# Second layer of a four-layer mixture-of-experts network: in every other slot VectorE casts the f32 gelu to fp16 in place of a second gelu on ScalarE

## The chip, the cores and the metric

The kernel runs on one core of one Trainium2 chip. The metric is the device time of one execution in microseconds (us). The engines are TensorE (PE in the profile; PEld is its weight load), VectorE (DVE), ScalarE (ACT), GpSimd (POOL) and SyncE (SP, here only the issuer of loads).

## The reference

Sixteen images of 64 channels and 24 x 24 pixels pass four layers. Each layer is `x = x + conv(layernorm(x))`, then `t = t + ffn(layernorm(t))` on the 9216 tokens of 64 channels. Each ffn routes a token to 2 of 8 experts. The second layer's ffn, which the change touches, is

```python
weights = top_p / top_p.sum(axis=-1, keepdims=True)
xe = xn[None, :, :] * ln_g[:, None, :] + ln_b[:, None, :]
h = jax.nn.gelu(jnp.einsum('end,edh->enh', xe, W1) + b1[:, None, :], approximate=False)
y = jnp.einsum('enh,ehd->end', h, W2) + b2[:, None, :]
out = (weights[:, :, None] * sel).sum(axis=1)
```

with 256 hidden units for each of 8 experts; `sel` is the rows of `y` of the two chosen experts. The first layer's ffn has the same form with 128 hidden units. Layers three and four have experts of 682 hidden units with a silu gate.

## The kernel before

The tokens are held in two halves of 4608 (36 tiles of 128). Layers one and two are computed densely: every expert for every token, and the routing weight (zero for six experts) multiplies the result. Layers three and four gather only the chosen rows, through tables in HBM that GpSimd's indirect DMAs fill. Precision is kept by splitting: a value goes into a matmul as an fp16 part and an fp16 remainder.

The dense part (`dense(l, h)`, one function for each engine) walks over *slots*. A slot is a span of 4 tiles (512 tokens), one expert, and one chunk `c` of 128 hidden units. Layer one has one chunk, layer two has two, `c = 0` and `c = 1`, and the two slots of an expert are a *unit* (called a pair below). A half of layer two has 72 units, 144 slots. In a slot `w`:

- PE (`up`, L1732 and L1733) makes 128 x 512 hidden values in one of three PSUM banks, two slots ahead of their use.
- ACT (L848) reads the bank twice: a gelu in f32 into `hid` (the two tiles `hb0`, `hb1` in turn), and the same gelu in fp16 into `hid_hl` (four tiles in turn, `hl0`, `hl1`, `act0`, `act1`). It must first see that VectorE is done with slot `w - 2` (semaphore `lo_ready`) since `hid` has two buffers, and that PE is done with slot `w - 4` (`down_ps`).
- DVE (`low`, L1435) writes the remainder, f32 minus fp16 part, into the second half of the fp16 tile.
- PE (`down`, L1748, 12 matmuls) multiplies both parts by the second weight; with `c = 0` it adds the bias first (L1742) and starts a new sum, with `c = 1` the sum is whole.
- DVE (`gated`) multiplies the unit's sum by the routing weights (L1452, into one of two buffers), and POOL (L688) adds this to `x`. In the second half from unit 32 on (`direct`), DVE itself multiplies and adds (L1446, four instructions), since POOL then scatters rows for layer three (L635).

The order on each engine is written out. DVE does `low(k)`, and after the `low` of the next unit's `c = 0` slot the `gated` of the unit before: `low(c=1)`, `low(c=0)`, `gated`, `low(c=1)`, and so on. Other work is woven between slots by a plan: in half 0 of layer two the weights of layer three are prepared in five pieces (ACT casts at L817 after a `c = 0` slot, DVE remainders at L1338), in the first 64 slots of half 1 the whole preparation of layer three's first half runs (layernorm, gate, routing, on DVE, ACT and PE). `link` makes DVE wait for its own last instruction by a semaphore, so that the next one reads finished data.

Of the kernel before, what the change touches and what calls it, by code (L numbers as in the profile page):

```python
# [28 lines left out]
P = 128  # L29
# [35 lines left out]
SPAN = 4  # L65
# [161 lines left out]
def program(nc, I, out):  # L227
    ctx = ExitStack()
    with ctx:
# [86 lines left out]
        hid = hb  # L316
# [5 lines left out]
        hid_hl = [t[:, :] for t in hl[0:2]] + [t[:, :].bitcast(FP16) for t in act]  # L322
# [71 lines left out]
        def unit_base(l, h):  # L394
            return n_of(l, h) * NUNIT

        def slot_base(l, h):

            return NUNIT * (h if l == 0 else HALVES + 2 * h)

        def slots(l):

            return [(s8, e, c) for s8 in range(NS) for e in range(E) for c in range(l + 1)]
# [7 lines left out]
        def weave(l, h):  # L411

            todo = {(0, 0): [FIRST + k for k in range(8)], (0, 1): [], (1, 0): [WPREP + k for k in range(3 * PIECES)],
                    (1, 1): stages(SPARSE)}[l, h]
            n = len(slots(l))
            used = n * 45 // 100 if (l, h) == (1, 1) else n - 4
            return [todo[min(len(todo), -(-(v + 1) * len(todo) // used)) - 1] if todo else -1 for v in range(n)]
# [3 lines left out]
        def direct(l, h, u):  # L421

            return (l, h) == (1, 1) and u >= PLACED
# [32 lines left out]
        def wait_from(eng, semaphore, value):  # L456

            if not isinstance(value, int) or value > 0:
                eng.wait_ge(semaphore, value)
# [244 lines left out]
        def _(a):  # L704
# [133 lines left out]
            def dense(l, h, aside):  # L838

                vb, plan = slot_base(l, h), weave(l, h)  # L840
                for v, (s8, e, c) in enumerate(slots(l)):
                    w = vb + v
                    a.wait_ge(s["up_ps"], w + 1)
                    wait_from(a, s["lo_ready"], w - 1)
                    wait_from(a, s["down_ps"], w - 3)
                    at = e * (l + 1) + c
                    for dst in (hid[w % 2], hid_hl[w % 4]):
                        ins = a.activation(dst[:, 0:SPAN * P], PB[w % 3][:, :], ACT.Gelu, scale=1.0 / WSCALE,  # L848
                                           bias=b1T[l][:, at:at + 1])
                    ins.then_inc(s["gelu_done"], 1)  # L850
                    aside.upto(plan[v])
                aside.upto(LAST)

            def moe(l):
# [44 lines left out]
                if l == SPARSE:  # L899
                    a.wait_ge(s["down_ps"], slot_base(1, 1) + len(slots(1)))  # L900
# [16 lines left out]
            for l in range(SPARSE):  # L917
                if l == 0:
                    side_by_side(Woven(prep(l, 0)), Woven(prep(l, 1)), ROUTE + 4, Woven(first_weights(0)))
                else:  # L920
                    side_by_side(Woven(prep(l, 0)), Woven(prep(l, 1)))
                for h in range(HALVES):
                    dense(l, h, Woven(after(l, h)))
# [9 lines left out]
        def _(v):  # L933
            turn = Turn()

            def link(ins):

                ins.then_inc(s["dve_chain"], 1)
                v.wait_ge(s["dve_chain"], turn(s["dve_chain"]))

            def bc(ap, m):

                return ap.unsqueeze(2).broadcast_to([ap.shape[0], ap.shape[1], m])
# [483 lines left out]
            def dense(l, h, aside):  # L1427

                vb, ub, plan, todo = slot_base(l, h), unit_base(l, h), weave(l, h), slots(l)

                def low(k):
                    w = vb + k
                    p = hid_hl[w % 4]
                    v.wait_ge(s["gelu_done"], w + 1)
                    v.tensor_tensor(p[:, SPAN * P:2 * SPAN * P], hid[w % 2][:, 0:SPAN * P], p[:, 0:SPAN * P], ALU.subtract  # L1435
                                    ).then_inc(s["lo_ready"], 1)

                def gated(k):
                    s8, e, c = todo[k]
                    u = s8 * E + e  # L1440
                    v.wait_ge(s["down_ps"], vb + k + 1)
                    if direct(l, h, u):
                        v.wait_ge(s["added"], ub + u)
                        for t_ in range(SPAN):
                            xt = x[h][:, s8 * SPAN + t_, :]
                            ins = v.scalar_tensor_tensor(xt, PB[3 + (ub + u) % 3][:, t_ * C:(t_ + 1) * C],  # L1446
                                                         gd[h][:, s8 * SPAN + t_, e:e + 1], xt, ALU.mult, ALU.add)
                        ins.then_inc(s["added"], 1)
                        return
                    wait_from(v, s["added"], ub + u - 1)  # L1450
                    g = gd[h][:, s8 * SPAN:(s8 + 1) * SPAN, e]
                    v.tensor_tensor(tg[u % 2].rearrange("p (t c) -> p t c", c=C),  # L1452
                                    PB[3 + (ub + u) % 3][:, 0:SPAN * C].rearrange("p (t c) -> p t c", c=C), bc(g, C), ALU.mult
                                    ).then_inc(s["gated"], 1)
                for k in range(len(todo)):
                    low(k)
                    if k > 0 and todo[k - 1][2] == l:
                        gated(k - 1)
                    aside.upto(plan[k])
                gated(len(todo) - 1)  # L1460
                aside.upto(LAST)
# [451 lines left out]
```

## Time and profile before

| what | value |
|---|---|
| median of 3 runs | 2053.25 us (2052.39 to 2055.82) |
| the profiled execution's own time | 2052.43 us |
| its span, first to last instruction | 2050.0 us |
| busy, share of the span: PE, DVE, ACT, POOL | 71%, 82%, 63%, 46% |
| layer two, half 0 | about 512 to 733 us |
| layer two, half 1, woven with layer three's preparation (32 units) | about 733 to 888 us |
| layer two, half 1, units 32 to 71 (direct) | about 888 to 980 us |

The profile is one execution. A row of the timeline gives start and duration; in square brackets is how long the engine stood idle before, and what ended it. Instructions of DVE and ACT that follow without a wait begin some hundredths of a microsecond before the one before them ends, so the cost of an instruction in a chain is the distance from start to start, not its duration. A few per cent of the records are missing.

### The profile page before, as it was taken

How to read it: one execution, taken by the hardware profiler on the slowest of the kernel's cores; microseconds unless marked ns; L12 is line 12 of the kernel's file. 1: busy time of each engine (PE TensorE's matmuls, PEld its weight loads, DVE VectorE, ACT ScalarE, POOL GpSimd, SP SyncE). 2: the span in 40 equal slices, each digit the busy share in tenths (PEclk: the TensorE clock that was granted, in tenths of full speed). 3: DMA queues.
4: the chain of work that ended last, by engine and by line, in shares of the span. 5: the costliest groups of instructions: out<-in, count | busy, mean ns of one | idle time of the engine just before them, and what ended most of it. 6: DMA issues, size and time to landing. Idle time of an engine off the chain costs nothing.

```text
span 2050.0 us, 47395 instructions
## 1 busy us (share of the span) xinstructions
PE 1463.0 (71%) x16020; PEld 1091.2 (53%) x16020; DVE 1689.1 (82%) x2916; ACT 1282.2 (63%) x2361; POOL 935.6 (46%) x899
## 2 busy tenths in 40 slices
PE   3658989526777776788339999996331449999994
PEld 2544444515333343444238888885220248888883
DVE  5676788697778767888669999999868869999998
ACT  1026989313898867689218888887320128888883
POOL 1003778100222211257117777656215757777653
PEclk9856899676899877789559999998555569999997
DMA  7000000000000100000001111210300011111212
GB/s 321 1 0 28 2 29 2 0 0 0 29 29 29 48 10 1 1 18 27 12 8 42 41 43 43 81 31 11 129 0 16 22 32 41 42 41 40 79 33 97
DMA packets 49469, 74.97 MB, mean 37 GB/s; under 512 B 13636, under 2 KB 34235, under 8 KB 46590
## 3 DMA queue, kind: packets, MB, share of 16 engines
q1 hardware_dynamic: 28354, 42.26, 6.7%
q0 software_dynamic: 20896, 29.73, 4.3%
q8 instruction: 146, 2.39, 0.5%
q14 instruction: 73, 0.60, 0.1%
HBM read 39.88 MB, written 33.08 MB: 36 GB/s over the span
## 4 chain that ended last, share of the span: by engine, by line
PE 36%; DVE 17%; issue 4%; ACT 3%; DMA 0%; POOLq 0%; POOL 0%; DVEq 0%; SPq 0%; ACTq 0%
PE bank L1806 13%; PE bank L1807 10%; PE bank L1823 5%; PE bank L1825 3%; DVE tmp L1161 2%; DVE x L1446 2%; PE bank L1678 1%; PE bank L1527 1%; PE bank L1777 1%; DVE xn L983 1%; DVE st L981 1%; DVE tmp L1134 1%; ACT hl L848 1%; DVE act L1435 1%; DVE xn L1002 1%
## 5 line engine op out<-in xcount | busy, mean ns | idle before, releaser
L688 POOL TENSOR_TENSOR x<-x,ysb 128x256 f32<-128x256 f32 x248 | 230.8, 931 | 639.8 <-DVE ysb L1452 622.5
L635 POOL DMA_INDIRECT rows<-rowsb,pos x288 | 307.5, 1068 | 207.6 <-DVE pos L1290 121.0
L848 ACT ACTIVATE hb<-bank,bias_sb 128x512 f32<-128x512 f32 x432 | 316.2, 732 | 99.7 <-PE bank L1733 52.1
L674 POOL DMA_INDIRECT y<-w,ids x256 | 283.7, 1108 | 138.0 <-DVE w L1359 73.1
L1806 PE MATMUL bank<-xT,uA_ 128*114 128x256 f16 x960 | 255.0, 283 | 5.7
L1807 PE MATMUL bank<-xT,uB_ 128*114 128x256 f16 x960 | 254.2, 277 | 0.0
L1806 PE MATMUL bank<-xT,gA_ 128*114 128x256 f16 x960 | 251.4, 288 | 3.5
L1369 DVE TENSOR_TENSOR act<-bank,act 114x512 f32<-114x512 f32 x320 | 219.9, 687 | 37.8 <-PE bank L1807 15.7
L865 ACT ACTIVATE act<-bank 114x512 f32<-114x512 f32 x320 | 191.1, 597 | 85.7 <-PE bank L1807 76.6
L1807 PE MATMUL bank<-xT,gB_ 128*114 128x256 f16 x960 | 238.1, 274 | 0.0
L1823 PE MATMUL bank<-dW_,hl 114*128 x1920 | 228.8, 220 | 3.0 <-DVE hl L1373 3.0
L1373 DVE TENSOR_TENSOR hl<-act,hl 114x512 f16<-114x512 f32 x320 | 218.7, 683 | 0.0
L1825 PE MATMUL bank<-dW_,hl 114*128 x1920 | 214.1, 192 | 0.0
L1435 DVE TENSOR_TENSOR hl<-hb,hl 128x512 f16<-128x512 f32 x216 | 162.3, 752 | 59.0 <-ACT hl L848 50.1
L1435 DVE TENSOR_TENSOR act<-hb,act 128x512 f16<-128x512 f32 x216 | 166.1, 769 | 42.6 <-ACT act L848 32.2
L873 ACT ACTIVATE hl<-act 114x512 f16<-114x512 f32 x320 | 199.1, 622 | 1.9 <-DVE act L1369 1.7
L1732 PE MATMUL bank<-rowsb,w 128*128 128x512 f16 x432 | 182.5, 423 | 4.6 <-DMA land<-land 3.9
L1733 PE MATMUL bank<-rowsb,w 128*128 128x512 f16 x432 | 182.8, 423 | 0.0
L1527 PE MATMUL bank<-K,xn 128*128 128x128 f32 x144 | 38.4, 412 | 193.3 <-DVE xn L1002 169.6
L1823 PEld LDWEIGHTS bank<-dW_,hl 114*128 114x128 f16 x1920 | 170.2, 97 | 6.6 <-issue 3.9
L1825 PEld LDWEIGHTS bank<-dW_,hl 114*128 114x128 f16 x1920 | 170.1, 98 | 0.0
L848 ACT ACTIVATE act<-bank,bias_sb 128x512 f16<-128x512 f32 x216 | 158.3, 733 | 0.0
(384 smaller groups left out, 3463.1 us busy)
## 6 DMA issues: line engine op xcount, KB each, us to landing
stage<-up SPq DMA_DIRECT2D x8, 1368.0 KB, 7.4
xs<-rows SPq DMA_DIRECT2D x160, 65.0 KB
rows<-land POOLq DMA_DIRECT2D x8, 1137.5 KB, 16.5
rows<-rowsb,pos POOLq DMA_INDIRECT x288, 2.3
y<-w,ids POOLq DMA_INDIRECT x256, 2.3
stage<-down SPq DMA_DIRECT2D x2, 1368.0 KB
rowsb<-y SPq DMA_DIRECT2D x4, 640.0 KB, 5.8
x<-tokens SPq DMA_DIRECT2D x2, 1152.0 KB, 7.3
```

Source lines behind the costliest of these rows:

```text
L635: pool.indirect_dma_start(rows_d[l - SPARSE], bass.IndirectOffsetOnAxis(pos[h][:, k, j:j + 1], 0), words(h)[:, j * RW // 2:(j + 1) * RW // ...
L674: pool.indirect_dma_start(y_d, bass.IndirectOffsetOnAxis(ids[:, t * SUB + u:t * SUB + u + 1], 0), ysb[r][:, u * C:(u + 1) * C], None, boun ...
L688: pool.tensor_tensor(xv, xv, tg[u % 2], ALU.add).then_inc(s["added"], 1)
L848: ins = a.activation(dst[:, 0:SPAN * P], PB[w % 3][:, :], ACT.Gelu, scale=1.0 / WSCALE, bias=b1T[l][:, at:at + 1])
L873: a.activation(hl[g][0:CH, 0:2 * ROWS], hold(k, g)[0:CH, :], ACT.Copy).then_inc(s["hi_ready"], 1)
L1369: v.tensor_tensor(p, PB[2 + q % 2][0:CH, :], p, ALU.mult).then_inc(s["prod_ready"], 1)
L1373: v.tensor_tensor(hl[g][0:CH, 2 * ROWS:4 * ROWS], hold(k, g)[0:CH, :], hl[g][0:CH, 0:2 * ROWS], ALU.subtract).then_inc(s["hp_ready"], 1)
L1435: v.tensor_tensor(p[:, SPAN * P:2 * SPAN * P], hid[w % 2][:, 0:SPAN * P], p[:, 0:SPAN * P], ALU.subtract).then_inc(s["lo_ready"], 1)
L1806: pe.matmul(PB[bank][0:CH, o], w[0][2 * g + c][:, at], xT[k][:, :], start=True, stop=False)
L1807: ins = pe.matmul(PB[bank][0:CH, o], w[1][2 * g + c][:, at], xT[k][:, :], start=False, stop=True)
L1823: pe.matmul(y[:, o:o + 2 * C], hl[g][0:CH, col:col + P], w, start=(g == 0 and c == 0 and u == 0), stop=False, skip_group_check=True)
L1825: ins = pe.matmul(y[:, o:o + C], hl[g][0:CH, 2 * ROWS + col:2 * ROWS + col + P], w[:, 0:C], start=False, stop=(g == G - 1 and c == 1), ski ...
```

## The change

In layer two, slots with `c = 1`, ACT computes only the f32 gelu. DVE makes the fp16 part by a `tensor_copy` from the f32 tile, waits for it through `link`, and subtracts as before.

```diff
+        def plain(l, c):
+
+            return l == 1 and c == 1
+
...
-                    for dst in (hid[w % 2], hid_hl[w % 4]):
+                    for dst in (hid[w % 2], hid_hl[w % 4])[0:1 if plain(l, c) else 2]:
                         ins = a.activation(dst[:, 0:SPAN * P], PB[w % 3][:, :], ACT.Gelu, scale=1.0 / WSCALE,
                                            bias=b1T[l][:, at:at + 1])
                     ins.then_inc(s["gelu_done"], 1)
...
                     v.wait_ge(s["gelu_done"], w + 1)
+                    if plain(l, todo[k][2]):
+                        link(v.tensor_copy(p[:, 0:SPAN * P], hid[w % 2][:, 0:SPAN * P]))
                     v.tensor_tensor(p[:, SPAN * P:2 * SPAN * P], hid[w % 2][:, 0:SPAN * P], p[:, 0:SPAN * P], ALU.subtract
                                     ).then_inc(s["lo_ready"], 1)
```

That is 144 gelus fewer on ACT and 144 casts more on DVE, 72 in each half. On DVE, in the direct stretch, where `L1435` is `low`, `L1446` is `gated` and `x1` is the second half's activations, the order before is

```order
L1435 TENSOR_TENSOR hl1<-hb1,hl1 128x512
L1435 TENSOR_TENSOR act0<-hb0,act0 128x512
L1446 SCALAR_TENSOR_TENSOR x1<-bank4,land,x1 128x64 x4
L1435 TENSOR_TENSOR act1<-hb1,act1 128x512
L1435 TENSOR_TENSOR hl0<-hb0,hl0 128x512
L1446 SCALAR_TENSOR_TENSOR x1<-bank5,land,x1 128x64 x4
```

and in the changed kernel, whose lines stand six further down (`low` is L1441, the cast L1440, `gated` L1452):

```order
L1440 CAST hl1<-hb1 128x512
L1441 TENSOR_TENSOR hl1<-hb1,hl1 128x512
L1441 TENSOR_TENSOR act0<-hb0,act0 128x512
L1452 SCALAR_TENSOR_TENSOR x1<-bank4,land,x1 128x64 x4
L1440 CAST act1<-hb1 128x512
L1441 TENSOR_TENSOR act1<-hb1,act1 128x512
L1441 TENSOR_TENSOR hl0<-hb0,hl0 128x512
L1452 SCALAR_TENSOR_TENSOR x1<-bank5,land,x1 128x64 x4
```

So the cast stands right behind `gated`, ahead of the `low` of a `c = 1` slot. The same holds in half 0 with a single `gated` instruction whose result POOL waits for. On ACT, in layer two, the changed kernel has three gelus for a unit where there were four:

```order
L852 ACTIVATE hb0<-bank0,bias_sb 128x512
L852 ACTIVATE act0<-bank0,bias_sb 128x512
L852 ACTIVATE hb1<-bank1,bias_sb 128x512
L852 ACTIVATE hb0<-bank2,bias_sb 128x512
L852 ACTIVATE hl0<-bank2,bias_sb 128x512
L852 ACTIVATE hb1<-bank0,bias_sb 128x512
```

Gone are the instructions that wrote `act1` and `hl1` behind each `hb1`. Nothing else moves on any engine.

## Rows read from the trace of the kernel before

**Rows 1.** Windows: us, busy time and instructions of each engine, granted clock, DMA.
```profile
512.00:733.00 221.00, 167.35 (x2107) 84.56 (x2105) 168.59 (x238) 191.54 (x313) 56.90 (x72) 0.88 0.09 33
733.00:888.00 155.00, 105.22 (x1037) 61.72 (x1038) 115.88 (x210) 98.63 (x149) 27.95 (x32) 0.71 0.00 1
888.00:980.00 92.00, 80.33 (x1142) 39.96 (x1139) 81.59 (x235) 90.35 (x156) 71.16 (x72) 1.00 0.09 26
```

**Rows 2.** Timeline of POOL, half 0: start, duration; first and last of five adds.
```profile
528.11 0.72 POOL L688 TENSOR_TENSOR x<-x,ysb 128x256 f32<-128x256 f32 x1 [1.77 <-DVE ysb L1452]
...
537.95 0.72 POOL L688 TENSOR_TENSOR x<-x,ysb 128x256 f32<-128x256 f32 x1 [1.77 <-DVE ysb L1452]
```

**Rows 3.** Timeline of DVE, half 0, one undisturbed unit and the next remainder.
```profile
528.26 1.12 DVE L1435 TENSOR_TENSOR hl<-hb,hl 128x512 f16<-128x512 f32 x1 [0.23 <-ACT hl L848]
529.42 0.69 DVE L1435 TENSOR_TENSOR act<-hb,act 128x512 f16<-128x512 f32 x1
530.03 0.42 DVE L1452 TENSOR_TENSOR ysb<-bank,land 128x256 f32<-128x256 f32 x1
530.77 1.04 DVE L1435 TENSOR_TENSOR act<-hb,act 128x512 f16<-128x512 f32 x1 [0.32 <-ACT act L848]
```

**Rows 4.** Timeline of ACT, the same place.
```profile
528.12 0.69 ACT L848 ACTIVATE hb<-bank,bias_sb 128x512 f32<-128x512 f32 x1
528.69 0.70 ACT L848 ACTIVATE act<-bank,bias_sb 128x512 f16<-128x512 f32 x1
529.47 0.69 ACT L848 ACTIVATE hb<-bank,bias_sb 128x512 f32<-128x512 f32 x1
```

**Rows 5.** Timeline of PE, the same place: the second matmuls of the first slot.
```profile
529.44 0.52 PE L1748 MATMUL bank<-w1d,hl 128*128 128x64 f16 x12 [0.45 <-DVE hl L1435]
```

**Rows 6.** Timeline of DVE, half 1, the direct stretch.
```profile
924.00 0.69 DVE L1435 TENSOR_TENSOR hl<-hb,hl 128x512 f16<-128x512 f32 x1 [0.23 <-ACT hl L848]
924.61 0.85 DVE L1446 SCALAR_TENSOR_TENSOR x<-bank,land,x 128x64 f32<-128x64 f32 x4
...
926.32 0.69 DVE L1435 TENSOR_TENSOR act<-hb,act 128x512 f16<-128x512 f32 x1 [0.26 <-ACT act L848]
```

**Rows 7.** DVE instructions with one SBUF input: timeline row; group row (busy, mean ns).
```profile
7.45 0.23 DVE L1479 CAST id<-K 128x128 f16<-128x128 f32 x1 [7.45 <-DMA K<-konst]
...
L1231 DVE TENSOR_SCALAR land<-lg 128x288 f32<-128x288 f32 x2 | 0.6, 310 | 0.1
```

**Rows 8.** Timeline of DVE: two instructions that `link` joins.
```profile
26.23 0.20 DVE L995 TENSOR_TENSOR st<-st 128x36 f32<-128x36 f32 x1
26.46 0.20 DVE L996 TENSOR_TENSOR st<-st 128x36 f32<-128x36 f32 x1
```

**Rows 9.** DVE and POOL at once: line L1415 (ns least/median/most), then timelines, half 0.
```profile
L1415 DVE TENSOR_SCALAR stage<-stage,bias_sb x8: 340/341/809, 188.6 to 190.9; 128x256 f32<-128x256 f32 x8
...
545.86 0.69 DVE L1435 TENSOR_TENSOR hl<-hb,hl 128x512 f16<-128x512 f32 x1
...
545.89 1.24 POOL L688 TENSOR_TENSOR x<-x,ysb 128x256 f32<-128x256 f32 x1 [4.00 <-DVE ysb L1452]
```

**Rows 10.** Timelines of layer one: ten POOL adds, and two neighbouring remainders on DVE.
```profile
339.48 11.42 POOL L688 TENSOR_TENSOR x<-x,ysb 128x256 f32<-128x256 f32 x10
...
340.37 0.69 DVE L1435 TENSOR_TENSOR act<-hb,act 128x512 f16<-128x512 f32 x1
...
341.53 0.69 DVE L1435 TENSOR_TENSOR act<-hb,act 128x512 f16<-128x512 f32 x1
```

**Rows 11.** Timeline of ACT, half 0: the weight casts of one piece.
```profile
555.72 2.68 ACT L817 ACTIVATE gA_<-stage 128x912 f16<-128x912 f32 x3
```

**Rows 12.** Groups of DVE, 733 to 888 us: busy, mean ns, idle before, releaser.
```profile
L1435 DVE TENSOR_TENSOR hl<-hb,hl 128x512 f16<-128x512 f32 x33 | 24.9, 756 | 8.8 <-ACT hl L848 8.4
L1435 DVE TENSOR_TENSOR act<-hb,act 128x512 f16<-128x512 f32 x32 | 23.5, 733 | 11.5 <-ACT act L848 11.2
L1452 DVE TENSOR_TENSOR ysb<-bank,land 128x256 f32<-128x256 f32 x32 | 13.4, 419 | 4.1 <-PE bank L1748 4.0
```

**Rows 13.** Timeline of POOL: the first scatter for the second half's rows.
```profile
1065.23 0.95 POOL L635 DMA_INDIRECT rows<-rowsb,pos  x1 [80.72 <-DVE pos L1290]
```

## The prediction

> **What bounds the kernel now.** I read three views in turn: the windows, to see which engine is full in each stretch of layer two; the timelines of one undisturbed unit, to see which wait ends last there; and the groups of the stretch where layer three's preparation is woven in.
>
> The windows [rows 1] part layer two in three. In half 0 ACT is busy 191.5 of 221 us and DVE 168.6. In the woven stretch nobody is full: DVE 115.9 of 155, ACT 98.6. In the direct stretch ACT is busy 90.4 of 92 and DVE 81.6, so ACT is the bound, with DVE close behind.
>
> In an undisturbed unit of half 0 the five adds of POOL stand 9.84 us apart over four units, 2.46 us a unit [rows 2]. ACT issues gelus 0.57 us apart (528.12 to 528.69), but the next one comes 0.78 later, at 529.47 [rows 4]. The reader is to see why: the remainder of the `c = 1` slot, which ACT has to see done, took 1.12 us instead of 0.69 and ended at 529.38 [rows 3]. POOL's add stood in the way; it ran from 528.11 to 528.83 [rows 2], and the remainder ended 0.55 after it. So a unit is four gelus of 0.58 and some waiting for a collision of DVE and POOL. In the direct stretch POOL does not add; a unit takes 926.32 - 924.00 = 2.32 us, four gelus, and DVE waits 0.23 to 0.26 us for ACT in each [rows 6].
>
> The change takes 0.58 us a unit from ACT, which then has three gelus (1.73 us) and is no bound any more. The question is what DVE's chain comes to with the cast in it.
>
> **The price of the cast.** No row has it at 512 columns. The nearest are two instructions with one SBUF input and an SBUF output: a cast of 128 columns took 0.23 us and an f32 scaling of 288 columns 0.31 [rows 7]. That is 0.08 us for 160 columns more, 0.0005 a column, and for 512 columns 0.23 + 384 x 0.0005 = 0.43 us. The other end is the remainder of the same 512 columns, which has two inputs, 0.69 [rows 3]. I take 0.43, since the row of the cast is the same operation with the same types. Then `link`: two linked instructions stand 0.03 us apart (26.23 + 0.20 to 26.46) [rows 8], while unlinked ones overlap by 0.08 (the `gated` at 530.03 begins before the remainder's end at 530.11) [rows 3]. So a cast in a full chain costs 0.43 + 0.03 = 0.46 us, since the remainder would have begun where the cast begins. [...]
>
> **Direct stretch, 40 units.** Count from the end of the remainder of a `c = 1` slot. The `c = 0` remainder begins 0.08 before and ends at 0.61. `gated` needs the matmuls: PE began 0.06 after that end (529.38 to 529.44) and took 0.52 [rows 3, 5], so with 0.03 for the signal `gated` begins at 0.61, where DVE alone would allow 0.53. Its four instructions take 0.85 less the overlap, 0.77 [rows 6]: 1.38. The gelu of the cast's slot is long there: ACT begins 0.09 after the remainder [rows 3, 4], 0.69 later it is done, at 0.78. Cast to 1.81, link to 1.84, remainder to 2.53. Against 2.32 that is 0.21 x 40 = **+8.4 us**. Without the wait for the matmuls it is 2.45 and +5.2; with a cast of 0.69 it is 2.79 and +18.8.
>
> **Half 0, 72 units.** The same to 0.61; one `gated` of 0.42 ends at 1.03; the cast begins at 0.95, before POOL asks (its add begins 0.08 after `gated`), and ends at 1.38. That a DVE instruction with one SBUF input and an add collide shows at L1415: 0.34 us as a rule, 0.81 once, in the midst of adds [rows 9]. An add that comes second ended 0.58 after the DVE instruction (545.86 + 0.69 = 546.55, 545.89 + 1.24 = 547.13) [rows 9]: here at 1.96. The remainder, second in its turn, ends 0.55 later: 2.51. So the collision is not gone, it only sits behind the cast, and a unit costs 2.51 against 2.46: 0.05 x 72 = **+3.6**. If the cast did not hold the add back, the add would end at 1.84 and the unit at 2.39: -5.0 instead.
>
> The weight casts on ACT [rows 11] blocked the gelus fully before. Now ACT is done with a `c = 0` slot at 0.61 + 0.09 + 0.57 + 0.69 = 1.96 and begins the next at 2.60, 0.64 idle, and that next gelu is 0.14 early (0.81 with its signal, needed at 0.95): 0.78 us of cover in four pieces (the first lies at the start): **-3.1**. DVE's own weight work costs what it did.
>
> **Woven stretch, 32 units.** Upper end: every cast on the path, 32 x 0.46 = +14.7. Lower end: every `c = 1` gelu on the path as well, 32 x (0.46 - 0.58) = -3.8. DVE is idle for 39 us [rows 1], 19.6 of them before remainders for ACT and 4.0 before `gated` for PE [rows 12], more than the casts need, but gathered in a few long waits. I take the middle of the ends, **+5**.
>
> **What follows layer two** is a chain that keeps its length. POOL's 72 scatters run beside the direct stretch; should casts hold some back, the next scatter waits 80.7 us for DVE [rows 13], so nothing is late.
>
> **Sum.** +8.4 + 3.6 - 3.1 + 5 = +13.9 on the profiled execution's 2052.43: **2066 us**. That execution is 0.8 below the median of the runs shown.
>
> **The rivals.**
> *Faster: POOL's add slips beside `gated`.* In layer one ten adds took 11.42 us, 1.14 each, in step with remainders 1.16 apart (340.37, 341.53) [rows 10]; there the add hides beside `gated`. If in half 0 the remainder follows the cast without POOL getting its turn, the unit is 0.95 + 0.43 + 0.03 + 0.69 = 2.10, and 72 x -0.36 = -25.9; with the other terms 2052.4 - 25.9 - 3.1 + 13.4 = 2037. It decides the sign once the unit is under 2.32 (10.3 us over 72). [...] Chance 0.10.
>
> [...] Chance 0.07.
>
> *No change: the woven stretch pays for the direct one.* With ACT on its path (-3.8) and `gated` not held by the matmuls (+5.2), +0.5 from half 0: +1.9, 2054. For it: two thirds of the waits there are before a remainder, for ACT [rows 12]. Against it: they stand mostly ahead of `c = 0` slots, whose two gelus stay. Chance 0.15.
>
> **How the numbers follow.** The forecast has 0.68; its own range, with the ends of the woven stretch and of the cast, is 2057 to 2082. For 8 in 10 the range takes in the third rival and half of the gap to the first: 2047 to 2082. What a measurement of this kernel can tell from no change is about 0.2%, 4 us. Slower by more: the forecast and the second rival, less a little at its lower end, 0.73. Faster: the first rival and the tail of the third, 0.13. Within: 0.14.
>
> **What would show it.** In the profile after: 144 casts of about 0.43 us; units 2.53 us apart in the direct stretch with ACT idle 0.5 us or more in each and no wait of DVE for ACT; in half 0 units 2.5 apart, adds of about 0.85 (begun at 1.11, ended at 1.96) and stretched remainders behind the casts; the end of layer two some 14 us later, and all after it as long as before. It is wrong if adds stay at 0.73 with units near 2.1, if the cast takes 0.7, or if PE, which waits more, shows a granted clock under 1.00 in the direct stretch.

## Result and profile after

The changed kernel takes 2072.99 us (median of 16 runs, 2057.78 to 2075.91) against 2054.72 us (16 runs of the kernel before, 2048.23 to 2057.07): a ratio of 1.0078, 95% interval 1.0062 to 1.0094, or 16 us, 13 to 19. It is slower, as forecast; 2066 us was forecast, 2047 to 2082. The 16 runs of the changed kernel lie 18 us apart: the shortest has the highest mean granted clock of TensorE among them, 0.830, the longest the lowest, 0.816.

The profiled execution of the changed kernel took 2074.41 us, its span is 2072.5 us, 22.5 more than before. Its lines are 4 to 6 higher than those of before: the cast is L1440, the remainder (`low`) L1441, `gated` L1452 and L1458, POOL's addition L692, the gelus L852.

First the windows of the changed kernel, cut at its own stages (us, busy time and instructions of PE, PEld, DVE, ACT and POOL, granted clock, DMA); before, they are [rows 1]:

```profile
518.00:737.00 219.00, 165.52 (x2090) 83.29 (x2088) 193.24 (x306) 152.51 (x235) 62.30 (x72) 0.89 0.09 34
741.00:902.00 161.00, 105.11 (x1028) 60.39 (x1029) 131.68 (x242) 81.87 (x117) 25.60 (x32) 0.71 0.00 1
904.00:1004.00 100.00, 79.17 (x1127) 39.48 (x1125) 97.45 (x277) 74.39 (x115) 70.04 (x74) 1.00 0.10 29
```

ACT was busy for 191.5 us in half 0 and is for 152.5; DVE goes from 168.6 to 193.2. In the direct stretch the two have changed places: ACT was full, now DVE is, 97.5 of 100 us.

Where the time went is read from four marks in the timeline: the first gelu of layer two, the last `gated` of half 0, the first four-instruction `gated` of the direct stretch, and the first reduction of the layer norm behind it. Kernel before:

```profile
512.64 0.69 ACT L848 ACTIVATE hb<-bank,bias_sb 128x512 f32<-128x512 f32 x1
...
728.39 0.42 DVE L1452 TENSOR_TENSOR ysb<-bank,land 128x256 f32<-128x256 f32 x1 [0.92 <-PE bank L1748]
...
889.50 0.85 DVE L1446 SCALAR_TENSOR_TENSOR x<-bank,land,x 128x64 f32<-128x64 f32 x4
...
980.94 1.22 DVE L981 TENSOR_REDUCE st<-x 128x16 f32<-128x1024 f32 x1
```

The same marks in the timeline of the changed kernel:

```profile
517.83 0.69 ACT L852 ACTIVATE hb<-bank,bias_sb 128x512 f32<-128x512 f32 x1
...
736.46 0.42 DVE L1458 TENSOR_TENSOR ysb<-bank,land 128x256 f32<-128x256 f32 x1 [0.62 <-PE bank L1754]
...
904.00 0.86 DVE L1452 SCALAR_TENSOR_TENSOR x<-bank,land,x 128x64 f32<-128x64 f32 x4
...
1003.91 1.22 DVE L985 TENSOR_REDUCE st<-x 128x16 f32<-128x1024 f32 x1
```

Half 0 goes from 215.75 to 218.63 us (+2.9), the part from its last `gated` to the direct stretch from 161.11 to 167.54 (+6.4), the direct stretch from 91.44 to 99.91 (+8.5): layer two is 17.8 us longer, 468.3 against 486.1. Behind it nothing is longer: 1069.1 us to the end of the span before, 1068.6 after.

The rest of the 22.5 us stands ahead of the first cast: the first gelu of layer two comes at 517.83 instead of 512.64, 5.2 later, behind layer one, whose code is the same. There the two executions were granted different clocks. One window of layer one, before:

```profile
250.00:300.00 50.00, 43.81 (x565) 21.36 (x561) 42.67 (x77) 43.72 (x76) 39.01 (x38) 0.97 0.09 30
```

and in the changed kernel:

```profile
250.00:300.00 50.00, 43.86 (x496) 21.05 (x495) 38.68 (x69) 39.22 (x67) 34.75 (x33) 0.83 0.08 29
```

Nearly all of it arises in this window: `gated` of layer one stands 0.3 us earlier than before at 267 us and 4.7 later from 284 on. In the twelve profiles of this study, all with the same layer one, that mark lies between 512.08 and 519.00 us. So two spans can differ by 7 us with no change; stage times from the marks are the better measure for effects of a few us, and the timed rounds go beside them. They vary too: half 0 with the same code in it takes 214.75 to 215.88 us in four of the profiles below, and the woven part without casts 160.33 to 162.55.

### The profile page after: what moved, and what is told of

Its sections match the earlier page's. It is cut to its first block, busy times and chain, and to the rows that moved or that the text cites. A ratio compares the mean times of both kernels' runs of the same rounds, so it can differ in the third digit from the quotient of the medians.

```text
span 2072.5 us, 47395 instructions
## 1 busy us (share of the span) xinstructions
PE 1469.9 (71%) x16020; PEld 1091.7 (53%) x16020; DVE 1749.9 (84%) x3060; ACT 1217.8 (59%) x2217; POOL 944.2 (46%) x899
## 4 chain that ended last, share of the span: by engine, by line
PE 36%; DVE 20%; issue 3%; ACT 1%; DMA 0%; POOLq 0%; POOL 0%; DVEq 0%; SPq 0%; ACTq 0%
PE bank L1812 13%; PE bank L1813 10%; PE bank L1829 5%; PE bank L1831 3%; DVE tmp L1165 2%; DVE x L1452 2%; DVE act L1441 2%; DVE hl L1441 1%; PE bank L1684 1%; PE bank L1533 1%; PE bank L1783 1%; DVE xn L987 1%; DVE st L985 1%; DVE tmp L1138 1%; DVE xn L1006 1%
## 5 line engine op out<-in xcount | busy, mean ns | idle before, releaser
L692 POOL TENSOR_TENSOR x<-x,ysb 128x256 f32<-128x256 f32 x248 | 234.8, 947 | 650.7 <-DVE ysb L1458 634.0
L852 ACT ACTIVATE hb<-bank,bias_sb 128x512 f32<-128x512 f32 x432 | 313.6, 728 | 182.2 <-PE bank L1739 96.9
L678 POOL DMA_INDIRECT y<-w,ids x256 | 288.7, 1128 | 129.5 <-issue 66.1
L1813 PE MATMUL bank<-xT,gB_ 128*114 128x256 f16 x960 | 242.7, 276 | 0.0
L1441 DVE TENSOR_TENSOR hl<-hb,hl 128x512 f16<-128x512 f32 x216 | 166.3, 770 | 23.9 <-ACT hl L852 14.5
L1441 DVE TENSOR_TENSOR act<-hb,act 128x512 f16<-128x512 f32 x216 | 167.6, 776 | 19.5 <-ACT act L852 9.8
L1829 PEld LDWEIGHTS bank<-dW_,hl 114*128 114x128 f16 x1920 | 169.6, 97 | 10.8 <-issue 5.4
L1812 PEld LDWEIGHTS bank<-xT,uA_ 128*114 x960 | 123.7, 129 | 50.3 <-issue 41.7
```

Source lines behind the costliest of these rows:

```text
L678: pool.indirect_dma_start(y_d, bass.IndirectOffsetOnAxis(ids[:, t * SUB + u:t * SUB + u + 1], 0), ysb[r][:, u * C:(u + 1) * C], None, boun ...
L692: pool.tensor_tensor(xv, xv, tg[u % 2], ALU.add).then_inc(s["added"], 1)
L1812: pe.matmul(PB[bank][0:CH, o], w[0][2 * g + c][:, at], xT[k][:, :], start=True, stop=False)
L1813: ins = pe.matmul(PB[bank][0:CH, o], w[1][2 * g + c][:, at], xT[k][:, :], start=False, stop=True)
L1829: pe.matmul(y[:, o:o + 2 * C], hl[g][0:CH, col:col + P], w, start=(g == 0 and c == 0 and u == 0), stop=False, skip_group_check=True)
```

## The experiments

Each kernel below is the changed kernel with another condition for the cast, or with another place of the addition, or both. All compute the whole reference. Their lines are one higher than those of the changed kernel (cast L1441, remainder L1442), since `plain` takes the half and the unit as well:

```diff
-        def plain(l, c):
+        def plain(l, h, u, c):
```

The table gives what all of them measured: stage times by the four marks (the first mark is that of each trace, a `gated` of four instructions counts from its first, "woven" is from the last `gated` of half 0 to the direct stretch), and the ratio to the kernel before in the same rounds.

| kernel | half 0 | woven | direct | sum | ratio (95%) |
|---|---|---|---|---|---|
| before | 215.75 | 161.11 | 91.44 | 468.3 | 1 |
| changed | 218.63 | 167.54 | 99.91 | 486.1 | 1.0078 (1.0062 to 1.0094) |
| cast_half0 | 218.60 | 162.37 | 91.36 | 472.3 | 1.0000 (0.9983 to 1.0016) |
| cast_woven | 215.88 | 167.87 | 91.20 | 475.0 | 1.0023 (1.0012 to 1.0033) |
| cast_direct | 214.79 | 161.39 | 99.90 | 476.1 | 1.0033 (1.0021 to 1.0044) |
| cast_direct_8th | 214.75 | 161.28 | 95.26 | 471.3 | 1.0016 (1.0004 to 1.0028) |
| cast_on_c0 | 215.41 | 165.43 | 96.82 | 477.7 | 1.0048 (1.0033 to 1.0063) |
| cast_not_behind_blocks | 213.57 | 170.27 | 99.91 | 483.8 | 1.0060 (1.0037 to 1.0082) |
| cast_behind_weight_casts | 211.44 | 161.07 | 91.35 | 463.9 | 0.9980 (0.9969 to 0.9991) |
| direct0_second_gelu | 211.44 | 162.55 | 91.47 | 465.5 | 0.9974 (0.9958 to 0.9990) |
| direct0_cast | 215.46 | 167.69 | 99.91 | 483.1 | 1.0069 (1.0044 to 1.0094) |
| direct0_cast_behind | 208.74 | 160.33 | 91.33 | 460.4 | 0.9944 (0.9927 to 0.9961) |

### One stage at a time

The cast in half 0 alone, in the woven units alone, in the direct units alone:

```diff
-            return l == 1 and c == 1
+            return l == 1 and c == 1 and h == 0
+            return l == 1 and c == 1 and h == 1 and not direct(l, h, u)
+            return l == 1 and c == 1 and direct(l, h, u)
```

cast_half0: 

> The cast only in half 0 of layer two (72 units), the second half as before. Forecast of the prediction: +3.6 us for the units and -3.1 us for the four weight casts, +0.5 us. Read from the trace of the change: from the first gelu of half 0 to its last addition 216.2 us before and 219.1 us after, so +2.9 us, because TensorE runs at its lower clock for some units behind each weight cast; by that the time is some +3 us. Rival (the whole shift of 8.1 us that the traces show at the end of half 0 belongs to the casts there): +8 us.

cast_woven: 

> The cast only in the first 32 units of the second half, where layer norm and routing of the next half are woven in. Forecast of the prediction: +5 us (ends -3.8 and +14.7). The traces of before and of the change: 148.9 and 155.2 us between the first and the last addition, +6.3 us. Rival (that stretch waits for other work and the traces differ by the clock alone): 0 to +2 us.

cast_direct: 

> The cast only in the last 40 units of the second half, where VectorE multiplies and adds itself. Theory: ScalarE sets the pace there before (30.00 of 30 us busy between 930 and 960 us) and VectorE after it (29.37 of 30 us), so a unit goes from 2.32 to 2.54 us and the time by +8.5 us, while the rest of the program stands. Rival (it pays back what another stretch gains, or the later start of the next stage hides it): under +4 us.

Each stage takes its longer time only where the casts are, and the other stages stay as before, within 1.3 us: the effects neither pay for each other nor hide. The rounds give +4.7 us (2.5 to 6.8) for the woven units and +6.8 us (4.3 to 9.0) for the direct ones, about the stage times' +6.8 and +8.5; the rivals of these two fall. For half 0 they give 0 us (-3.5 to +3.3), which excludes the rival's +8 and can't tell +0.5 from +2.9; there only the traces speak: 218.60 and 218.63 us in the two with all casts, against 214.75 to 215.88 in the four without. The rival's 8.1 us was a false reading: the end of half 0 carries the 5.2 us of layer one. Nor do the traces bear out the lower clock of TensorE behind each weight cast: in the 8 us behind ACT's five blocks the granted clock is 0.79, 1.00, 0.59, 0.79 and 0.57 in cast_half0, against 0.61, 0.79, 0.79, 0.79 and 0.57 before.

### The cast in the other slot

```diff
-            return l == 1 and c == 1
+            return l == 1 and c == 0
```

cast_on_c0: 

> The whole change with the cast in the c = 0 slots in place of the c = 1 slots. The working of the prediction: the multiplication waits for the matmuls of the c = 1 slot only because nothing of VectorE's lies between but one remainder; with the cast in between that wait (0.08 us a unit) is gone, and a unit of the direct stretch takes 2.46 in place of 2.54 us: 98.9 us for the stretch instead of 102.1. In half 0 the cast is no longer right behind VectorE's blocks (-2.4 us), but the slot behind ScalarE's weight casts again has two gelus (+2.6 us). Together -3 us against the changed kernel, still slower than before. Rival (VectorE is not what sets the unit, or the wait for the matmuls only moves): 2.54 us and no difference.

Timeline of the direct stretch, ACT and DVE:

```profile
940.62 0.69 DVE L1442 TENSOR_TENSOR hl<-hb,hl 128x512 f16<-128x512 f32 x1
...
941.23 0.85 DVE L1453 SCALAR_TENSOR_TENSOR x<-bank,land,x 128x64 f32<-128x64 f32 x4
...
942.60 0.42 DVE L1441 CAST act<-hb 128x512 f16<-128x512 f32 x1
942.76 0.69 ACT L853 ACTIVATE hb<-bank,bias_sb 128x512 f32<-128x512 f32 x1 [0.59 <-PE bank L1740]
...
943.66 0.85 DVE L1453 SCALAR_TENSOR_TENSOR x<-bank,land,x 128x64 f32<-128x64 f32 x4
```

A unit is 2.43 us here (941.23 to 943.66), in other places 2.53; the stretch takes 96.82 us, 3.1 less than with the cast in `c = 1`, as expected. The multiplication begins 0.08 us before the remainder ends, so nothing waits for the matmuls, and what is left is DVE's own sum: the prediction's 2.45 "without the wait for the matmuls". ACT idles 0.59. The rest of the expectation missed: half 0 was to stay as it was and is 3.2 us shorter, the woven part 2.1. The slot behind ACT's weight casts has two gelus again, so the intervals of POOL's additions across these blocks were to go back up; three of the four are 3.74 us, where the kernel before has 4.87 and the changed kernel 4.12 to 4.42. Why was not tried. The kernel is still slower than before.

### Fewer casts in the direct stretch

```diff
-            return l == 1 and c == 1
+            return l == 1 and c == 1 and direct(l, h, u) and u % 4 == 1
```

cast_direct_8th: 

> The cast in one slot of eight (one unit of four) of the direct stretch alone, the second gelu everywhere else. If the two engines' busy times set the pace, a group of four units has ScalarE at 4 x 2.32 - 0.58 = 8.70 us and VectorE at 4 x 2.08 + 0.46 = 8.76 us, 2.19 us a unit against 2.32: 40 x -0.13 = -5 us against the kernel before. Rival (two buffers of the f32 gelu are too few to even out the slots, each slot with a cast costs its own 0.2 us): 10 x +0.2 = +2 us.

The theory fell. Timeline around one of the ten casts:

```profile
933.03 0.72 ACT L853 ACTIVATE hb<-bank,bias_sb 128x512 f32<-128x512 f32 x1
...
934.00 0.69 ACT L853 ACTIVATE hb<-bank,bias_sb 128x512 f32<-128x512 f32 x1 [0.25 <-PE bank L1740]
934.58 0.42 DVE L1441 CAST act<-hb 128x512 f16<-128x512 f32 x1
...
935.81 0.69 ACT L853 ACTIVATE hb<-bank,bias_sb 128x512 f32<-128x512 f32 x1 [0.54 <-issue]
936.34 0.86 DVE L1453 SCALAR_TENSOR_TENSOR x<-bank,land,x 128x64 f32<-128x64 f32 x4
```

ACT saves 0.58 us and then stands idle for 0.25 and 0.54: it cannot run ahead, since it waits for PE's next sums and then, by the code, for the remainder that frees one of two f32 buffers. Two units of four take 2.53 us, two take 2.32, so one cast costs 0.42 us, nearly its whole price, against 0.21 where every unit has one, and twice what the rival gave it. The stretch is 3.8 us longer than before, and the rounds say +3.3 us (0.8 to 5.8). Busy times of two engines don't average over units here. That the two buffers are the reason is read from these waits; no kernel with more buffers was run.

### Behind DVE's blocks of weight remainders

In half 0 five blocks of DVE make the remainders of layer three's weights: four at L1338 (before; three instructions, 3.66 us) and a fifth at L1343 (six instructions, 4.22 us). Timeline of one, kernel before:

```profile
623.00 3.66 DVE L1338 SCALAR_TENSOR_TENSOR uB_<-stage,uA_ 128x912 f16<-128x912 f32 x3
...
626.59 0.68 DVE L1435 TENSOR_TENSOR act<-hb,act 128x512 f16<-128x512 f32 x1
...
627.32 0.52 PE L1748 MATMUL bank<-w1d,act 128*128 128x64 f16 x12 [3.29 <-DVE act L1435]
...
628.42 0.82 PE L1748 MATMUL bank<-w1d,hl 128*128 128x64 f16 x12
```

and the same block in the changed kernel:

```profile
628.40 3.66 DVE L1342 SCALAR_TENSOR_TENSOR uB_<-stage,uA_ 128x912 f16<-128x912 f32 x3
...
631.99 0.41 DVE L1440 CAST act<-hb 128x512 f16<-128x512 f32 x1
632.43 0.69 DVE L1441 TENSOR_TENSOR act<-hb,act 128x512 f16<-128x512 f32 x1
...
633.18 0.82 PE L1754 MATMUL bank<-w1d,act 128*128 128x64 f16 x12 [3.63 <-DVE act L1441]
```

Before, ACT's second gelu was long done when the block ended. Now the cast is queued behind the block: the remainder begins 0.37 us after the block's end, where it began 0.07 before it, and PE idles 3.63 us instead of 3.29. Before, PE's first twelve matmuls took 0.52 us and the next twelve 0.82; now the first twelve take 0.82 already. The windows behind the block show the granted clock. Kernel before:

```profile
626.50:629.00 2.50, 1.68 (x27) 1.14 (x28) 2.14 (x5) 1.65 (x3) 0.62 (x1) 0.89 0.23 64
629.00:632.50 3.50, 3.50 (x36) 1.64 (x33) 2.85 (x4) 2.92 (x6) 0.83 (x2) 0.59 0.36 154
```

and changed:

```profile
632.00:634.50 2.50, 1.32 (x14) 0.77 (x14) 2.15 (x6) 0.69 (x1) 0.00 (x0) 0.64 0.23 64
634.50:638.00 3.50, 3.50 (x30) 1.81 (x29) 2.62 (x5) 1.95 (x3) 0.87 (x2) 0.50 0.39 169
```

In the 3 us after these windows the clock is 1.00 before and 0.75 in the changed kernel. So PE's clock falls behind the block in both kernels, over 3.5 us to 0.59 before and to 0.50 in the changed kernel; with the cast it is low from the first matmuls on (0.64 for 0.89) and for longer, and DVE then waits for PE. The units around the block (intervals of POOL's additions) took 5.22, 2.89 and 2.75 us before and take 5.98, 3.42 and 2.86, at a pace of 2.46 and 2.51: 3.5 us over the pace became 4.7. Over all five blocks it is 19.9 and 22.3. The experiment takes the cast away there:

```diff
-            return l == 1 and c == 1
+            return l == 1 and c == 1 and not (h == 0 and u % 14 == 9)
```

cast_not_behind_blocks: 

> The whole change, but without the cast in the five units of half 0 whose c = 1 slot comes right behind VectorE's 3.66 us blocks of weight remainders (units 9, 23, 37, 51, 65); there the second gelu stays. Theory: behind a block the cast stands on the path while TensorE is idle, so the stall around a block (its units over the steady pace, five together) grew from 19.9 to 22.4 us; without these casts it goes back to about 20, and half 0, from its first gelu to its last addition, takes 216.7 us instead of 219.1, the time -2.5 us against the changed kernel. Rival (the longer stalls are only the lower clock of that execution): 219 us and no difference.

Half 0 takes 213.57 us, 5.1 less than with all casts, twice what was expected. The units around a block take 5.23, 2.81 and 2.75 us, the five together 17.2 us over the pace against 22.3 with the casts, so the five cost 5.1 us, not 2.5. The windows behind the same block, without its cast:

```profile
627.40:629.90 2.50, 1.75 (x28) 1.12 (x29) 2.45 (x6) 1.44 (x3) 0.68 (x1) 0.93 0.25 59
629.90:633.40 3.50, 3.50 (x31) 1.48 (x29) 3.15 (x5) 2.22 (x4) 0.99 (x2) 0.56 0.38 161
```

The clock is not the whole of it. In the 8 us behind each of the five blocks the granted clock is 0.79, 0.79, 0.57, 0.62 and 0.59 in the changed kernel, and 0.79 behind all five without these casts; cast_half0 repeats the five numbers of the changed kernel within 0.01. Behind the first two, where it is the same, the units around the block take 0.65 us longer with the cast; behind the other three 1.5, 1.4 and 1.0. So the cast's own place on the path is some 3.3 us of the 5.1 (an estimate, five times 0.65), and the rest goes with the lower clock. Why it stays low behind three of the blocks was not tried.

Against the kernel before, the stalls without these casts are 2.7 us shorter (17.2 for 19.9). Of that 0.8 is the pace taken off (2.51 for 2.46, sixteen units), and 0.8 differs between executions of one code (cast_woven, with the same half 0 as the kernel before, has 19.9 too, cast_direct and cast_direct_8th have 19.1); the rest is open. The woven stretch, with no edit in it, was 2.7 us longer than in the changed kernel, and the intervals of the two ratios overlap, so the total does not show the gain; the stage does.

### Behind ACT's weight casts

The other half of that stage: the five slots behind ACT's own blocks (L817, 2.7 us for the one of [rows 11]), and no cast elsewhere.

```diff
-            return l == 1 and c == 1
+            return l == 1 and c == 1 and h == 0 and u % 14 == 0
```

cast_behind_weight_casts: 

> The kernel before with the cast in five slots only: those of half 0 that come right behind ScalarE's weight casts (c = 1 slots of units 0, 14, 28, 42, 56). The term of the prediction alone: there the second gelu is on the path and VectorE is idle, so each cast saves 0.78 us less what the next units give back. The intervals of the additions around these blocks, 4.87 us before, go to 4.1 us; half 0 is 3 us shorter (212 us), the time -3 us. Rival (TensorE's lower clock gives the gain back in the units behind): under 1 us.

Half 0 takes 211.44 us, 4.3 less than the kernel before (3.3 less than the 214.75 of cast_direct_8th, whose half 0 is unchanged too), and the rounds say -4.1 us (-6.4 to -1.8). Here the cast is a gain: DVE is idle, and the second gelu stands between ACT's block and the next remainder. The interval across the block goes from 4.87 us to 4.28, 4.30 and 4.53 in three of the four, and from 5.42 to 4.86 in the last; 4.1 was expected. The four intervals from each of these blocks are 2.0 us shorter in all. Another 1.4 lies around DVE's blocks, where nothing was changed, and 0.8 of that is in cast_direct as well, so what is plainly these casts' own is some 2 us.

### Without GpSimd's additions in half 0

`direct` is extended to half 0: DVE multiplies and adds, POOL adds nothing, and the waits count one half of `gated` fewer.

```diff
-            return (l, h) == (1, 1) and u >= PLACED
+            return (l, h) == (1, 0) or (l, h) == (1, 1) and u >= PLACED
...
-                    pool.wait_ge(s["gated"], ub + u + 1)
+                    pool.wait_ge(s["gated"], ub - (NUNIT if (l, h) == (1, 1) else 0) + u + 1)
```

With no cast (`plain` false):

direct0_second_gelu: 

> No cast at all; instead VectorE multiplies and adds itself in half 0 too, as it does in the last 40 units of the second half, and GpSimd adds nothing there. If the collision of VectorE and GpSimd is what keeps a unit at 2.46 us in place of four gelus, a unit takes 2.32 us: 72 x -0.14 = -10 us against the kernel before, some 2044 us, faster than both kernels. Rival (VectorE, with 0.43 us more a unit, and its 3.66 us blocks become the bound): 2.45 us or more a unit, 0 to +3 us.

With the cast in all 144 slots:

direct0_cast: 

> The whole change and, besides, VectorE multiplies and adds itself in half 0 too, so that GpSimd's additions and their collision are gone there. If VectorE's own work sets the pace with the cast, a unit of half 0 costs what one of the direct stretch costs, 2.54 against 2.51 us, and the time stays within +3 us of the changed kernel's: taking the collision away gives nothing, since the additions cost VectorE as much. Rival (the collision behind the cast is the whole price of half 0): units of 2.40 us, -8 us.

Without the cast an undisturbed unit takes 2.32 us (one multiplication at 530.43, the next at 532.75), as expected, but half 0 only gains 4.3 us of the 10, and the rounds say -5.3 us (-8.6 to -2.1). The stalls around DVE's blocks are longer: 5.42, 3.42 and 2.76 us at a pace of 2.32 is 4.7 us over, against 3.5 before.

With the cast the undisturbed unit takes 2.54 us. So the pace goes from 2.51 to 2.54 when POOL's additions are gone: DVE's own additions cost as much as the collision did, as expected. What the collision alone costs this kernel does not show. Half 0 as a whole is 3.2 us shorter than the changed kernel's, again by its stalls (5.60, 3.07 and 2.69 us around the third block, where the changed kernel has 5.98, 3.42 and 2.86). The ratios of the two overlap.

The last kernel joins the two gains: `direct` in half 0, and the cast in the five slots behind ACT's blocks alone.

direct0_cast_behind: 

> No cast but in the same five slots behind ScalarE's weight casts, and VectorE multiplies and adds itself in half 0. If both gains add up, half 0 takes 211.4 - 3 = 208.4 us and the time is -8 us against the kernel before, some 2047 us, the fastest of all. Rival: the gain behind the blocks is given back as TensorE's lower clock, 211 us and no better than without any cast.

Timeline of DVE behind one of ACT's blocks:

```profile
601.77 0.43 DVE L1441 CAST hl<-hb 128x512 f16<-128x512 f32 x1 [1.67 <-ACT hb L853]
602.23 0.69 DVE L1442 TENSOR_TENSOR hl<-hb,hl 128x512 f16<-128x512 f32 x1
```

DVE stood idle for 1.67 us before the cast, so the cast displaces no work of DVE's there. Half 0 takes 208.74 us, 7.0 less than before (208.4 was expected), and the kernel 2044.06 us: 0.9944 (0.9927 to 0.9961), faster than both kernels, and than the one before by 11.5 us (8 to 15).

## Why the prediction was right

**The direct stretch** was worked out to 2.53 us a unit. Timeline of the changed kernel:

```profile
930.61 0.69 DVE L1441 TENSOR_TENSOR act<-hb,act 128x512 f16<-128x512 f32 x1
931.22 0.69 DVE L1441 TENSOR_TENSOR hl<-hb,hl 128x512 f16<-128x512 f32 x1
...
931.36 0.52 PE L1754 MATMUL bank<-w1d,act 128*128 128x64 f16 x12 [0.49 <-DVE act L1441]
931.39 0.69 ACT L852 ACTIVATE hb<-bank,bias_sb 128x512 f32<-128x512 f32 x1 [0.31 <-issue]
931.92 0.86 DVE L1452 SCALAR_TENSOR_TENSOR x<-bank,land,x 128x64 f32<-128x64 f32 x4
932.36 0.69 ACT L852 ACTIVATE hb<-bank,bias_sb 128x512 f32<-128x512 f32 x1 [0.28 <-PE bank L1739]
932.70 0.42 DVE L1440 CAST hl<-hb 128x512 f16<-128x512 f32 x1
...
933.15 0.69 DVE L1441 TENSOR_TENSOR hl<-hb,hl 128x512 f16<-128x512 f32 x1
```

The working comes out row by row, counted from the end of the `c = 1` remainder at 931.30: the `c = 0` remainder ends at 0.61, the matmuls begin at 0.06, `gated` at 0.62, the cast at 1.40, the next remainder at 1.85, and the unit closes at 2.54 (930.61 to 933.15). In [rows 6] DVE waited for ACT in each unit; now ACT waits, 0.31 and 0.28. The cast takes 0.42 us (0.23 + 384 x 0.0005 is 0.42; the prediction wrote 0.43), and the link costs 0.03 (932.70 + 0.42 to 933.15). Forecast +8.4, measured +8.5. Two unlinked remainders overlap by 0.08 here (930.61 + 0.69 to 931.22). With such an overlap in place of the 0.03 the unit would be 2.43, an estimate from these rows; the trace has it at 2.54, so the overlap is lost.

**Half 0's pace** was worked out to 2.51. Timeline of the changed kernel, DVE and POOL:

```profile
528.26 1.10 DVE L1441 TENSOR_TENSOR hl<-hb,hl 128x512 f16<-128x512 f32 x1
...
529.28 0.68 DVE L1441 TENSOR_TENSOR act<-hb,act 128x512 f16<-128x512 f32 x1
...
529.98 0.42 DVE L1458 TENSOR_TENSOR ysb<-bank,land 128x256 f32<-128x256 f32 x1
530.32 0.42 DVE L1440 CAST act<-hb 128x512 f16<-128x512 f32 x1
...
530.48 0.84 POOL L692 TENSOR_TENSOR x<-x,ysb 128x256 f32<-128x256 f32 x1 [1.67 <-DVE ysb L1458]
530.77 1.10 DVE L1441 TENSOR_TENSOR act<-hb,act 128x512 f16<-128x512 f32 x1
```

The cast begins before POOL asks; the addition ends at 531.32, 0.58 after the cast; the remainder ends at 531.87, 0.55 after the addition. One remainder to the next is 2.51 us, against 2.46 [rows 2]. That ends two rivals. The addition does not slip beside `gated` (2.10 us and 2037). Nor do the two follow one another in full, the second rival with its chance of 0.07 (1.38 + 0.73 + 0.69 = 2.80 and 2087). No run shows that: 0.58 and 0.55 are less than the 0.73 and 0.69 that they take alone.

**The cover behind ACT's weight casts** was put at -3.1. The stalls there, each counted over the pace until the pace is back, come to 13.4 us before (such as 4.87, 2.87 and 2.71 at a pace of 2.46) and 10.8 after (such as 4.12, 3.00 and 2.74 at 2.51), -2.6; and taken alone these casts are a gain, some 2 us at these slots (cast_behind_weight_casts).

**The step that was mis-sized** is the sentence "DVE's own weight work costs what it did". Forecast 0; the stalls around the five blocks grew by 2.4 us over the kernel before, because the cast is queued behind each block while PE idles, and because behind three of them the granted clock over 8 us is 0.57 to 0.62, where it was under 0.79 behind two before (0.62 and 0.57). Taken away alone, these casts were worth 5.1. With the 2.4 half 0 is 3.6 - 2.6 + 2.4 = +3.4 instead of +0.5; the marks say +2.9, and up to +3.9 against the other executions with the same half 0 as before. The rule of naming what is queued behind a long instruction was kept for ACT and not for DVE.

**The woven stretch** was taken in the middle of wide ends, +5; it is +6.4. The working gives the two ends and not the +5, so that it came near is luck. The groups of DVE there, 741 to 902 us of the changed kernel (busy, mean ns, idle before, releaser), beside [rows 12]:

```profile
L1441 DVE TENSOR_TENSOR act<-hb,act 128x512 f16<-128x512 f32 x32 | 25.5, 797 | 5.6 <-ACT act L852 4.8
L1441 DVE TENSOR_TENSOR hl<-hb,hl 128x512 f16<-128x512 f32 x32 | 25.3, 790 | 2.7 <-ACT hl L852 2.0
...
L1440 DVE CAST hl<-hb 128x512 f16<-128x512 f32 x17 | 7.1, 419 | 0.8 <-ACT hb L852 0.7
L1440 DVE CAST act<-hb 128x512 f16<-128x512 f32 x16 | 7.1, 444 | 2.3 <-ACT hb L852 2.3
```

The casts add 14.2 us. The waits before remainders fall from 20.3 to 8.3, with 3.1 now before casts: so 8.9 us of idle time took most of the casts up, and not all. The third rival, in which this stretch pays for the direct one, fell with both its halves: +6.4 for -3.8, and the multiplication is held by the matmuls. Its "two thirds of the waits" is half: 19.6 of 39 us.

**The sum** of the stages, 2.9 + 6.4 + 8.5 = 17.8 us, is near the 18.3 between the medians and within the 13 to 19 of the ratio, against 13.9 forecast. Of the missing 3.9, 2.4 is the blocks of DVE and 1.4 the woven stretch. The profiled execution's further 5.2 us lie in layer one and were not part of the change. The granted clock in the direct stretch stayed at 1.00.

## What to carry to other kernels

Moving an instruction from the busiest engine to the next one gains, as far as busy times go, at most the gap between the two. And a stage whose engines pass two buffers round need not average: one moved instruction in eight slots cost nearly all of its duration. Find instead the slots where the receiving engine stands idle behind a block of the giving one; five casts there went with a gain of 4 us where all 144 lost 16. And cut both traces at marks before subtracting them: the end of a stage carries whatever came before it.

## What was not expected of the hardware

A cast of 0.42 us behind one of DVE's blocks made the stall 1.2 us longer. PE's idle time grew from 3.29 to 3.63 us, and its first twelve matmuls then took 0.82 instead of 0.52 us: the granted clock was 0.64 in the 2.5 us behind the block and 0.50 in the 3.5 us after them, where it had been 0.89 and 0.59. Behind the first two blocks the clock over 8 us was 0.79 with the cast as without (cast_not_behind_blocks). And executions of one program are granted the clock differently in the same stretch, 0.97 and 0.83 in one window of layer one, which moved what stands behind it by some 5 us.
